# A fused transformer block: self attention with the pair sums in the later tile, its projection and maxima dealt out step by step, and the value sums of two key tiles issued together in three groups of four

## What is computed

```python
qkv = x_norm @ W_qkv + b_qkv                                  # 512 x 512 per sequence, 16 heads of 32
attn_w = softmax(einsum('bhqd,bhkd->bhqk', q, k) * scale)      # 512 x 512 per head
attn_out = einsum('bhqk,bhkd->bqhd', attn_w, v) @ W_proj + b_proj
x = x + gate_a[:, None] * attn_out
```

## Time and profile before

| what | value |
|---|---|
| median of 3 runs | 2470.44 us (2468.13 to 2471.92) |
| the profiled execution's own time | 2474.41 us |
| its span | 2472.6 us |
| TensorE busy | 2372.6 us, 96% |
| VectorE, ScalarE, GpSimd busy | 1378.9, 1016.3, 607.2 us |
| granted TensorE clock, mean | 0.990 |
| QKV stage | about 474 to 779 us of the span |
| self attention | about 779 to 1376 us |

### The profile page before, as it was taken

The page is one execution under the profiler, slowest core; times in us unless marked ns, Lnnn a source line. Parts: engine busy times, 40 slices in busy tenths (PEclk is TensorE's granted clock), DMA queues, the critical chain, the costliest instruction groups (busy, mean ns, idle before and its releaser), DMA issues.

```text
span 2472.6 us, 32517 instructions
## 1 busy us (share of the span) xinstructions
PE 2372.6 (96%) x12056; PEld 1666.6 (67%) x12056; DVE 1378.9 (56%) x2471; ACT 1016.3 (41%) x1799; POOL 607.2 (25%) x509
## 2 busy tenths in 40 slices
PE   6889999999999999999998899999999999999999
PEld 5666667688786344444444567776788888888887
DVE  6566665744565877778776477666542222322221
ACT  3344544523233655555554344444442233233232
POOL 2002111200001766767766311212101101101100
PEclk9999999999999999999999999999999999999999
DMA  7697897645745554555651688877421110110110
GB/s 245 195 247 208 218 247 207 206 166 192 222 178 167 146 126 120 133 146 140 153 149 58 168 226 215 222 202 210 149 62 46 60 57 4 60 60 1 60 43 18
DMA packets 261324, 354.20 MB, mean 143 GB/s; under 512 B 61027, under 2 KB 109243, under 8 KB 261166
## 3 DMA queue, kind: packets, MB, share of 16 engines
q1 hardware_dynamic: 259998, 348.27, 50.2%
q0 software_dynamic: 1168, 3.85, 0.4%
HBM read 233.78 MB, written 116.69 MB: 142 GB/s over the span
## 4 chain that ended last, share of the span: by engine, by line
PE 81%; DVE 8%; ACT 4%; DMA 3%; issue 3%; SPq 1%; POOL 0%; ACTq 0%; DVEq 0%; POOLq 0%
PE banks L403 43%; PE banks L2263 14%; PE banks L1961 5%; PE banks L1983 4%; PE banks L1940 4%; PE banks L2003 3%; PE banks L1362 2%; PE banks L361 2%; PE banks L1376 2%; PE banks L1383 2%; DVE negated_max L1875 1%; DVE negated_max L1261 1%; DMA q_parts_self<-out_parts 1%; DVE heads_float L1901 1%; ACT self_exponentials L2047 1%
## 5 line engine op out<-in xcount | busy, mean ns | idle before, releaser
L2047 ACT ACTIVATE self_exponentials<-banks 128x512 f32<-128x512 f32 x512 | 285.6, 594 | 269.3 <-PE banks L1961 112.8
L1875 DVE TENSOR_REDUCE negated_max<-banks 128x1 f32<-128x512 f32 x512 | 330.2, 677 | 92.1 <-PE banks L1940 90.8
L1840 POOL TENSOR_TENSOR self_exponentials<-self_exponentials,self_exponentials 128x512 f32<-128x512 f32 x252 | 320.0, 1299 | 166.9 <-ACT self_exponentials L2047 166.9
L2263 PE MATMUL banks<-mlp_w_down_hi,out_parts 128*128 128x512 f32 x1024 | 333.8, 389 | 0.1
L344 POOL TENSOR_SCALAR norm_rstd<-norm_mean_var 128x4 f32<-128x4 f32 x32 | 8.0, 250 | 1301.1 <-DVE norm_mean_var L323 1301.1
L2220 DVE TENSOR_TENSOR out_parts<-wide,out_parts 128x512 fp32r<-128x512 f32 x128 | 92.9, 726 | 370.7 <-ACT out_parts L2292 370.7
L2282 ACT ACTIVATE wide<-banks,bias_columns 128x512 f32<-128x512 f32 x128 | 88.3, 690 | 426.0 <-PE banks L403 426.0
L1961 PE MATMUL banks<-self_query_stack,self_key_stack 98*128 98x512 f32 x512 | 232.3, 457 | 10.1 <-ACT self_exponentials L2047 7.2
L1961 PEld LDWEIGHTS banks<-self_query_stack,self_key_stack 98*128 98x128 f32 x512 | 96.5, 189 | 193.8 <-ACT self_exponentials L2047 159.2
L2263 PEld LDWEIGHTS banks<-mlp_w_down_hi,out_parts 128*128 128x128 f32 x1024 | 192.2, 188 | 40.5 <-DVE cross_last_x_rows L1305 0.5
L1940 PE MATMUL banks<-self_key_stack,self_query_stack 96*128 96x512 f32 x512 | 205.7, 405 | 9.1 <-DVE negated_max L1875 9.1
(11 more groups left out here) (209 smaller groups left out, 5232.7 us busy)
## 6 DMA issues: line engine op xcount, KB each, us to landing
L_query_stack<-q_parts_L SPq DMA_DIRECT2D x96, 256.0 KB, 4.9
norm_x<-x SPq DMA_DIRECT2D x24, 1024.0 KB, 7.9
self_query_stack<-q_parts_self SPq DMA_DIRECT2D x96, 256.0 KB, 4.0
self_key_stack<-k_parts_self SPq DMA_DIRECT2D x96, 256.0 KB, 6.3
cross_query_stack<-q_parts_cross SPq DMA_DIRECT2D x96, 256.0 KB, 5.0
x_rows<-x SPq DMA_DIRECT2D x23, 1024.0 KB, 5.9
x<-x_rows SPq DMA_DIRECT2D x22, 1024.0 KB, 5.4
q_parts_L<-out_parts SPq DMA_DIRECT2D x32, 512.0 KB, 4.8
```

The lines of the kernel that those rows point to most:

```text
L1840: e.tensor_tensor(self.p[kt - 1][:, h, :], self.p[kt - 1][:, h, :], self.p[kt][:, h, :], ALU.add).then_inc(self.paired.sem, 1)
L1875: e.tensor_reduce(k.nm[n % 2][:, h * NT + t:h * NT + t + 1], k.bank[:, self.max_banks.of["max", i], :], AX_X, ALU.max, negate=True).then_i ...
L2047: e.activation(self.p[kt][:, h, :], k.bank[:, self.scores.of["score", i], :], ACT.Exp, scale=SCALE).then_inc(self.exp.sem, 1)
L2263: mm = e.matmul(bank, l, w, start=j == 0 and q == 0, stop=j == JC - 1 and q == 2)
```

## The change

1. GpSimd writes the pair into the later tile, `p[kt]`, after V of the later tile. S reads it there. ScalarE's tiles 0 and 2 then wait for the pair head by head and no longer for S; tiles 1 and 3 wait for S.
2. `values_at`: in groups with g = 0 the bursts stay one V at a time. In groups with g = 1, 2, 3, V of tiles 0 and 1 are both issued after r9, and V of tiles 2 and 3 after r1 of the next group, with S between them (V S V); the bursts after r5 and r13 go away.
3. `PROJECT_STEPS`: the 16 pieces are spread: g = 1 in r3, r7, r11, r15; g = 2 in r2, r3, r6, r7, r10, r11, r14, r15; g = 3 in r3, r7, r10, r11.
4. `MAXIMA_STEPS`: maxima in g = 0 by 0, 1, 1, 2, 0, 1, 1, 2 and then one a step. The maxima of group 2 move from before group 0 into group 0. The QKV stage takes 35 steps of the self attention (its last two sequences) instead of 51, and the first three fetches come one sequence later. The ones rows of the last key buffer are set at group 1, not 0.
5. At the end of the stage, the last two V are issued together.

```diff
+def paced(counts, generator):
+    for count in counts:
+        for _ in range(count):
+            next(generator, None)
         yield
...
-                if b >= B - 3:
-                    weave(some(2 if b == B - 1 else 1, following))
+                if b >= B - 2:
+                    weave(some(b - B + 3, following))
...
+    PROJECT_STEPS = ((0,) * 16, (0, 0, 0, 1) * 4, (0, 0, 1, 1) * 4, (0, 0, 0, 1, 0, 0, 0, 1, 0, 0, 1, 1, 0, 0, 0, 0))
+    MAXIMA_STEPS = ((0, 1, 1, 2) * 2 + (1,) * 8, (1,) * 16, (1,) * 16, (1,) * 16)
...
+    def values_at(self, n, kt):
+        alone, before = SEQ[n][1] == 0, SEQ[n - 1][1] == 0
+        if kt == 0:
+            return ([(n - 1, 3)] if before else [(n - 1, 2), (n - 1, 3)]) if n else []
+        return ([(n, 0)], [(n, 1)], [(n, 2)])[kt - 1] if alone else ([], [(n, 0), (n, 1)], [])[kt - 1]
...
-        yield from braid(s.maxima(2), after(4, s.max_rows(1)))
...
-                tiles = (0, 1, 2, 1)[g]
-                part = after(4 if g == 1 else 0, some(tiles * 4, projecting))
-                side += [part] * tiles
+                side.append(paced(self.PROJECT_STEPS[g], projecting))
...
-        s.values(LAST - 1, NT - 1)
+        for kt in (NT - 2, NT - 1):
+            s.values(LAST - 1, kt)
...
-            pool.wait_ge(*self.av(n * NT + kt - 1))
+            pool.wait_ge(*self.av(n * NT + kt))
             for h in range(GH):
-                e.tensor_tensor(self.p[kt - 1][:, h, :], self.p[kt - 1][:, h, :], self.p[kt][:, h, :],
+                e.tensor_tensor(self.p[kt][:, h, :], self.p[kt][:, h, :], self.p[kt - 1][:, h, :],
                                 ALU.add).then_inc(self.paired.sem, 1)
...
-                tiles = (2 * j,)
+                tiles = (2 * j + 1,)
...
+                pair = 2 * (n - 1) + kt // 2
                 if n > 0:
-                    act.wait_ge(*self.paired((2 * (n - 1) + kt // 2) * GH + GH - 1))
-                    act.wait_ge(*(self.av((n - 1) * NT + kt) if kt % 2 else self.summed(2 * (n - 1) + kt // 2)))
+                    act.wait_ge(*(self.summed(pair) if kt % 2 else self.av((n - 1) * NT + kt)))
...
+                    if n > 0 and kt % 2 == 0:
+                        act.wait_ge(*self.paired(pair * GH + h))
```

More of the change, by code:

```diff
@@ L1542, in run @@
                 next(turning, None)
-                if b >= B - 3:
-                    weave(some(2 if b == B - 1 else 1, following))
+                if b >= B - 2:
+                    next(following)
                 yield
@@ L1547, in run @@
             turning = loading(b + 2)
-            if B - 6 < b < B - 3:
+            if B - 5 < b < B - 2:
                 next(following)
@@ L1739, in run @@
             if g > 0 and b > 0:
[L1740 to L1742 removed]
+                side.append(paced(self.PROJECT_STEPS[g], projecting))
             if n >= LAST - len(self.AHEAD):
                 side.append(some(self.AHEAD[n - LAST], following))
[L1745 to L1746 removed]
+            asking = paced(self.MAXIMA_STEPS[g], s.maxima(n + self.MAX)) if n < LAST - self.MAX else None
+            yield from braid(s.attend(n), s.finish(n - 1) if n else None, asking,
+                             after(2, s.max_rows(n + self.ROWS)) if n < LAST - self.ROWS else None, *side)
             if g == 0 and b > 0:
                 s.load_base(b - 1)
[L1749 removed]
+        for kt in (NT - 2, NT - 1):
+            s.values(LAST - 1, kt)
         s.sum_pair(LAST - 1, 1)
@@ L1858, in fetch @@
         def fetch(n):
-            if n >= 4:
+            if n == 3 or n > 4:
                 return
-            for done in self.freed_stack[n]:
+            i = min(n, 3)
+            for done in self.freed_stack[i]:
                 dve.wait_ge(*done)
-            e.memset(raw(self.keys[n][ST:ST_MAX]), 1.0).then_inc(self.key_ones.sem, 1)
+            e.memset(raw(self.keys[i][ST:ST_MAX]), 1.0).then_inc(self.key_ones.sem, 1)
         def maxima(n):
@@ L1964, in attend @@
                     if h == 1:
-                        if kt:
-                            values(n, kt - 1)
-                        elif n:
-                            values(n - 1, NT - 1)
+                        for tile in self.values_at(n, kt):
+                            values(*tile)
         def values(n, kt):
@@ L2003, in sum_pair @@
                     mm = e.matmul(k.bank[h * HD:(h + 1) * HD, bk, :], k.ones[:], self.p[kt][:, h, :],
-                                  start=kt == 0, stop=kt == tiles[-1] and j == 1)
+                                  start=j == 0, stop=kt == tiles[-1] and j == 1)
             mm.then_inc(self.summed.sem, 1)
```

5 lines of the change are left out of this document (2 added, 3 removed).

## The result

The changed kernel takes 2485.2 us (median of 4 runs, 2483.0 to 2487.9) against 2469.4 (4 runs), a ratio of 1.0058, 95% interval 1.0045 to 1.0070. It is 15.8 us slower; forecast was 2457.5 and faster.

What follows compares the result with a forecast made beforehand. TensorE, busy 96% of the span, was taken as the bound, with 6.7 us of waits a sequence. Terms -9.8 - 3.7 - 1.6 + 2.1 + 0.5 - 0.1 made about -13, so a median of 2457.5 us; range 2437 to 2475.

Steps and rivals of the forecast that it cites:

- QKV, -3.7: QKV stage: the maxima of group 2 leave this gapless stage, 16 x 0.234 = 3.7 us less.
- Group 0 at full clock: Group 0: more TensorE work from maxima keeps the clock full, 2 bursts x 0.85 = -1.6 us (bound 0).
- V S V, 2.74: Merged burst on TensorE: estimated at 0.88 + 0.88 + 0.98 = 2.74 us.
- S's wait in g = 1, 0.95: S in g = 1 stalls for GpSimd's pair, queued behind the bias adds: 0.95 us (0 to 1.5) per sequence.
- The half after r9, 9.05: Burst after r9 to burst after r1': VectorE's later chain makes it 9.05 us (8.4 to 9.7), against 8.1.
- g = 3, 18.3: Group g = 3 of a sequence: 2.74 + 5.7 + 9.9 = 18.3 us.
- g = 2, 19.4: Group g = 2 of a sequence: 2.74 + 6.97 + 9.7 = 19.4 us.
- g = 1, 17.56: Group g = 1 of a sequence: 1.86 + 5.7 + 0.95 + 9.05 = 17.56 us, against 21.39.
- Fewer bursts: the floor: TensorE per sequence: six of sixteen bursts go, lowering its floor by 0.7 + 1.2 = 1.9 us.
- g = 0, 17.1: Group g = 0 of a sequence: one V more in its first burst, the rest as now, 17.1 us.
- starvation of the product: Rival: VectorE's product waits for all four GpSimd adds, once a sequence: +12 us, 2482 us; chance 0.16.
- No gain: Rival: VectorE sets the pace in all halves after r9, +1.6 us a sequence; -3 in all, 2467 us; chance 0.20.

Runs made afterwards that it cites:

- part 4 alone: Kernel before with only the moves at the start of the stage (maxima of group 2, first fetches, ones rows): 2469.3 us, ratio 0.9985.
- spreading the bias adds: GpSimd's four bias adds of g = 1 put one each in r2, r6, r10, r14: changed kernel 2477.4 us (1.0025); changed kernel with single bursts 2453.2 us (0.9932).
- S first: Changed kernel with S ahead of both V in the merged bursts (S V V instead of V S V): 2487.0 us, ratio 1.0069.
- merging it alone: Fastest kernel (single bursts, earlier tile, spread pieces, start moves, bias adds spread; 2446.0 us) with merged bursts in g = 2 only: 2447.8 us, ratio 0.9897.
- pieces spread: Kernel before with only the projection's pieces spread (PROJECT_STEPS); pair in the earlier tile, bias adds as before: 2453.5 us, ratio 0.9931.
- 0.9895: Changed kernel with single bursts, bias adds spread and the pair in the earlier tile again: 2446.0 us, the fastest.
- 0.9955: Changed kernel, merged bursts kept, with the pair in the earlier tile again and bias adds spread: 2458.4 us.
- Parts 1, 3 and 4 together: Changed kernel with the value sums one by one in all groups (part 2 undone): 2468.0 us, ratio 0.9986.
- the later tile alone: Kernel before with only the pair written to the later tile, bursts, pieces, maxima and fetches as before: 2473.8 us, ratio 1.0010.
- the run with g = 3 merged alone: Fastest kernel (2446.0 us) with merged bursts in g = 3 only: 2459.6 us, ratio 0.9945.
- merged bursts in the earlier tile: Changed kernel with the pair in the earlier tile again (part 1 undone), merged bursts kept: 2462.4 us, ratio 0.9969.

## Why the prediction was wrong

Its sum said -13 us; the result is +16. By its own steps:

- **QKV, -3.7:** right (303.9 to 300.2; part 4 alone -3.7 in all). Group 0 at full clock: the clock held, but the gain went into a wait of 0.64 us for the row maxima's transfer and a slower start, so of the -1.6 only -0.3 was there.
- **V S V, 2.74:** right (2.71). **S's wait in g = 1, 0.95:** right (3.65 - 2.71 = 0.94), and with the cause given: spreading the bias adds removed it. (The prediction writes five V S V a sequence and adds up six; the 22.2 is right.)
- **The half after r9, 9.05:** right in size (9.14), and the collision of product and pair was as described (1.28, forecast to the end of the current add; 25 of the 31 products took over 1 us). So was the way from the product through the rounding and the exponential of r15 to the burst: 1.86 us, forecast 1.8. But the reason that I gave for the product's time, a chain starting 0.88 us later, fell with S first. What sets it is VectorE's work behind 1.83 us in which a merged burst lets it run dry. With S first the transpose came 0.85 us earlier and the product no earlier, so that the forecast distance of 4.0 us between the two held here was luck.
- **g = 3, 18.3, g = 2, 19.4, and g = 1, 17.56: mis-sized.** g = 3 took 18.9 even where the clock held (its half after r9 10.4, forecast 9.9), g = 2 19.7, g = 1 18.0 (its first gap 6.0, forecast 5.7). In g = 2 the floor was to fall by two bursts; merging it alone gave 0.2 us a sequence at best. The 1.9 us a sequence of "Fewer bursts: the floor" are not there: V S V saves 0.15 against S V and V, and the gap of eight steps with twelve products takes 7.1 to 7.2 us, at least twice the gap of four steps with six (3.48), so the 0.20 for each burst that goes were not saved.
- **g = 0, 17.1: the step that failed.** It took 19.4 (17.56 in group 4, where the clock held). I had asked of the granted clock only in group 0, where the earlier trace rows showed it fallen, and priced it at nothing everywhere else, though my own sum put a stall at r1' of g = 3 into every sequence. The stretched bursts cost 2.1 us a sequence: 1.8 in the bursts (10.7 over six), 0.3 in the last products ahead of them. That is 12.6 us, over half of the 24 us by which the six sequences missed (76.4 against 72.4), and the hand-over lost clock as well: from the last group to the end +6.8, forecast +0.9, of which at most 5.1 are the clock (0.50 for 13.7 us of the first 75, against 3.4 before). Less the clock a sequence took 74.3: the gain of 1.6 was not there either.
- **The rivals:** starvation of the product, the rival on the slower side, did not happen: no product waited for four adds, the longest took 1.38 us. The result came near its 2482 by another mechanism. "No gain" had the right engine and, less the clock, nearly the right sequence (74.3 against 74.0 before); it lacked the clock.

The price of the clock stood in the kernel before, at the one product that took 5.08 us. TensorE waited 4.01 us behind it, and then a single burst, S V, took 3.57 us instead of 1.86, at a granted clock of 0.50:

```profile
1305.84 0.76 PE L1940 MATMUL banks<-self_key_stack,self_query_stack 96*128 96x512 f32 x1 [4.01 <-DVE negated_max L1875]
...
1307.45 1.94 PE L2003 MATMUL banks<-self_exponentials,ones 128*32 128x512 f32 x8
1309.16 1.93 PE L1983 MATMUL banks<-self_exponentials,self_values 128*32 128x512 f32 x8
```

```profile
1305.84:1311.02 5.18, 5.18 (x19) 1.36 (x20) 5.11 (x7) 1.49 (x3) 4.70 (x4) 0.50 0.01 2
```

The prediction priced this event at 4.1 us, the wait alone; the 1.7 us behind it were left out.

What each part is worth, by the runs: pieces spread -17 us (the one large gain: g = 1 takes 18.2 us instead of 21.4, g = 2 and 3 give 1.5 back); moves at the start -3.7; later tile +2.5 alone, +9 where the pieces are spread and the bias adds out of the way (0.9932 against 0.9895), +17 with merged bursts; merging +15 to +23 (0.9955 against 0.9895, and 1.0025 against 0.9932). Parts 1, 3 and 4 together give 0.9986 where their sum would be 0.9926. Spreading the bias adds gives 13 of these 15 us back (0.9932), so they are the pair behind the bias adds, some 2.75 us in g = 1 of a sequence. It is not the later tile alone that brings this out: with the earlier tile and spread pieces S still waited 1.1 to 1.6 us there, where the rows of the bias adds landed late. In the changed kernel S waits 1.8 us less than with single bursts, and its bias adds waited for no DMA.

How much of merging is idle VectorE and how much clock: less what the stretched bursts added, a sequence with bias adds spread takes 73.2 us merged and 71.8 with single bursts (later tile), and 71.7 against 71.4 (earlier tile). So 1.4 and 0.7 us are the clock, and what is left, 1.4 and 0.3, goes to VectorE.

**Open.** That the clock falls after TensorE's wait at r1' is an association: stretched bursts were 6, 6, 5 and 4 of 6 at waits of 1.5 to 1.7 us, 3, 2, 2 and 1 at 1.2 to 1.3, none at 0.8 or less. But in the changed kernel the same wait of 1.50 us at the end of group 3 (g = 3 of the first sequence, without pieces) was followed by a burst of 2.72 us, and the run with g = 3 merged alone had the same wait of 1.24 as the others with fewer stretched bursts. What else has to come together was not settled. A merged burst is not needed for a fall: the kernel before lost its clock behind the wait of 4.01 us ahead of a single burst, and the later tile alone behind waits of 1.44 and 0.67 us (up to 1305.96; the next V, a single one, took 1.86 instead of 1.00). Nor is a wait of over a microsecond: with merged bursts in the earlier tile, and in g = 2 alone, the clock fell once each behind a wait of 0.68 and 0.69 us at the end of group 2, and V S V took 3.93. No run had a long wait at r1' of g = 3 ahead of a single burst, so at that place the two were not separated.

## What to carry over

Uniting bursts of one engine saves little for that engine (0.15 us here for each) and takes away the time in which the others were fed: look at what the engine that consumes its products does during the longer burst, for its idle time comes back in full if it sets the pace afterwards. Where a change puts a stall into a stream that is otherwise gapless (here 1.2 to 1.7 us), ask what it does to the granted clock behind it, look for such a stall in the kernel before, and give that a price. Where a row names what ended a wait, check by the kernel that the instruction waits for it at all. And when an instruction gets one more wait, look at what is already queued ahead of it on its engine: here four bias adds cost nothing until shorter groups and a later V made the pair behind them late, and part of that was a DMA that the adds themselves waited for.

## What was not expected of the hardware

- A VectorE product with both inputs in SBUF of 128 columns took 0.89 us beside GpSimd's adds and 0.28 at its shortest, one of 512 columns 1.28, and 0.67 without them. The extra 0.6 us does not shrink with the instruction. By the Trainium skill, "SBUF — State Buffer", section "SBUF: two separate sides", such an instruction and one of GpSimd exclude each other as a whole; the two sizes agree with that.
- Behind a wait of 1.68 us in an otherwise gapless stream the granted clock fell in each of six sequences, and V S V took 3.78 to 5.28 us instead of 2.71. With waits of 0.8 us or less at that place it never fell (eight kernels with single bursts there), though elsewhere it did behind 0.68.
- A wait inside a burst hardly shows in the busy time. Behind GpSimd's adds the products of S's four heads started 0.57, 1.23 and 1.22 us apart instead of together, and their records (0.6 us each, two for each head) left idle rows of only 0.17 and 0.18 us. So TensorE's busy time was 19.75 of 20.10 us in a group that took 17.11 with the bias adds spread.
